# The attention layer of a four-layer graph network on one NeuronCore: heads on 96 rows, division after the running sums, paired 64-row products

## The chip, the cores and the metric

The kernel runs on one NeuronCore of a Trainium2 chip. The core has TensorE (PE, matrix products, with its weight loads shown as PEld), VectorE (DVE), ScalarE (ACT), GpSimd (POOL) and SyncE (SP, which here only issues DMAs). The metric is the time of one execution on the device, in microseconds. All data is 32-bit floating point, and every product on TensorE shows as two records in the trace; a transpose is one record.

## The reference

There are N = 50000 nodes with 64 scalars and 32 vectors of 3 components (D = 160 numbers) and E = 25000 edges, sorted by destination. Four layers follow one another (0 to 3), each with a part over edges and a part over nodes. Only layer 1, the attention layer, is touched (and the setup of the weights). It computes for every edge:

```python
s_n, v_n = layernorm of the scalars, RMS norm of the vectors of both end nodes
msg_s = (s_n @ Ws_src)[src] + (s_n @ Ws_dst)[dst]         # vectors alike
w1 = rbf @ W_rbf                                          # 16 radial numbers per edge
m1_s, m1_v = tensor_product(msg_s, msg_v, y0, y1, w1)     # y: 4 numbers per edge
a = sum over 16 of leaky_relu(m1_s @ W_alpha) * alpha_dot # one logit for each of 4 heads
amax = segment_max(a, dst);  ex = exp(a - amax[dst])
den = segment_sum(ex, dst);  alpha = ex / (den[dst] + 1e-16)
val_s, val_v = m1_s @ Ws_val, (m1_v @ Wv_val) * sigmoid(val_s @ Wg);  val_s = sigmoid(val_s)
m2_s, m2_v = tensor_product(val_s, val_v, y0, y1, w2)
h = [m2_s @ Ws_vlin, m2_v @ Wv_vlin]                      # 4 heads, 64 scalars, 32 vectors
agg = segment_sum(alpha * h, dst)
out = node + [agg_s @ Wps, agg_v @ Wpv]
```

## The kernel before

The edge part of the attention layer works on groups of 512 edges (`GE`), 50 groups (`NG`). After two transposes the features lie on partitions and the 512 edges along the free dimension, so a matrix product is 64 to 128 rows by 512 columns and a segment sum is a scan along the free dimension, carried from group to group. Sums of a destination are complete at its last edge; only that column's row is scattered to the table `aggregates`.

The groups are pipelined by hand. `steps1` runs a body for every step `s`, unrolled for the first 8, in a loop of two steps after that, and unrolled for 5 more at the end. In step `s` the engines work on several groups at once: group `s` is gathered, `s-1` is normalised (layer norm), `s-2` goes through the first products, `s-3` through values, gates and the logits, `s-4` through the softmax sums. Each engine carries out its own list of instructions in order, and semaphores (one for each kind of work, counted by group) tie the lists together. The names and lines are:

- **PE** (`attn_tensor`): transposes `NT0` to `NT2` (L872) of `normed`; products `MS`, `MV`; `AV` (logit inputs and values), `VV`, `GT`; `XS`, `XV`, `GS`, `GV`, which spread the 4 rows of `ex` and `dec` (partitions 64 to 67) over 64 and 96 rows; six products of `z_rows` (`B1` to `G`, 64 rows each); `PS`, `PV`; `US` (logits in its rows 64 to 67), `UV`; transposes R0 (L933) and R1 (L935) back; `HS`, `HV`. All products are recorded at L859, in the helper `mm`. Results go to one of 8 banks of PSUM; `ORDER` gives each name a place, place modulo 8 is its bank, and `bank_free` waits until the last user of the bank has been read.
- **DVE** (`attn_vector`): adds `h_s`, `h_v` (L958, L961); `z_rows` (L966); softmax on 4 rows: scan of the denominator `den` (L975), +1e-16 (L978), `dec` = den - ex (L979), reciprocal (L981), `ex` and `dec` times the reciprocal (L984, L985); layer norm statistics (L992, L993, L1000, L1004 to L1011); leaky ReLU (L1016); gate (L1022), `vy` (L1028); weighting (L1034, L1037) and the running sums, which are already normalised (L1042, L1048, with the decay in PSUM); the six products `pr` (L1059); `normed` (L1066); `neg` (L1073), running maximum (L1080) and its differences (L1084 to L1089); `xs_y`, `xv_y` (L1094, L1097).
- **ACT** (`attn_scalar`): copies from PSUM (`nt`, `m_s`, `m_v`, `val`, `us`, `uv`), tanh, the vector part of `normed` (L823), the exponentials (L838, L840), the copies into `agg_out` (L846, L847).
- **POOL** (`attn_gpsimd`): reciprocal root of the variances (L755, a power of -0.5), copies of indices (L763, L764, L780), eight gathers (L771) and four scatters (L785) for a group.
- **SP** (`attn_sync`): loads `z_in` (radial numbers and y rows, 256 KB) and `y_big` (768 KB) for each group.

The setup at the start of the program loads and scales the weights, zeroes the table `aggregates` (38 MB, from ACT's DMA queue) and builds `goes_on` (L429: 1 where an edge has the destination of the one before it) from 50 row loads of SP; layer 0 begins when that is done.

## Time and profile before

| | before |
|---|---|
| median of 3 runs | 5688.06 us (5687.17 to 5689.68) |
| profiled execution: time / span | 5691.12 us / 5689.3 us |
| PE busy | 4587.4 us, 81% of the span |
| DVE busy | 4072.7 us, 72% |
| POOL busy | 3297.1 us, 58% |
| ACT busy | 2192.9 us, 39% |
| mean granted clock of TensorE | 0.817 of full speed |

A busy share is an average over all stages. The edge part of layer 1, the only one that the change rewrites, reaches from 1311 us (first gather) to 3276 us (last scatter); the page's 40 slices of 142 us show where the engines are full, and windows, timelines and groups cut to that stretch show how one step goes. The granted clock is the share of its pulses that TensorE gets: 1.00 is 2.4 GHz, 0.50 is 1.2 GHz.

### The profile page before, as it was taken

The numbers are of one execution on the slowest core, as the hardware profiler recorded it, in microseconds if no ns is written. First come the engines' busy times: TensorE is split into PE (matmuls) and PEld (weight loads), VectorE is DVE, ScalarE is ACT, GpSimd is POOL, SyncE is SP. The second block draws the span as 40 slices with busy tenths as digits, with TensorE's granted clock in tenths as the row PEclk, the third lists the DMA queues.
The fourth block names the chain that finished last, engine by engine and source line by source line (L and its number), as shares of the span: only waits on it lengthen the run. The fifth ranks groups of instructions, "written<-read, shape, count | busy, mean of one in ns | idle before, by whom it ended". The sixth has DMA issues, their size and how long they took to land. (4 is left out here: it accounts for less than half of the span.)

```text
span 5689.3 us, 73586 instructions
## 1 busy us (share of the span) xinstructions
PE 4587.4 (81%) x14104; PEld 2009.0 (35%) x14104; DVE 4072.7 (72%) x10653; ACT 2192.9 (39%) x5204; POOL 3297.1 (58%) x3685
## 2 busy tenths in 40 slices
PE   0699987776999999999999900888879788887665
PEld 0233335552333333333333200333347533334554
DVE  1466659996887888787788787444459855556999
ACT  0223325553222222222222256333349833334555
POOL 0366669995344434443443244666657666667998
PEclk9999988787777777777777755898989899898877
DMA  9222227662222222122212199222249722225665
GB/s 363 81 67 67 68 56 226 215 216 71 52 56 52 53 52 56 51 54 51 56 50 50 28 344 339 62 66 66 66 136 356 275 63 69 66 67 152 196 192 162
DMA packets 545392, 678.01 MB, mean 119 GB/s; under 512 B 57166, under 2 KB 387106, under 8 KB 545052
## 3 DMA queue, kind: packets, MB, share of 16 engines
q1 hardware_dynamic: 451888, 496.01, 28.4%
q0 software_dynamic: 86400, 142.71, 9.1%
q10 hardware_dynamic: 7020, 38.40, 1.6%
q8 instruction: 25, 0.41, 0.0%
q14 instruction: 59, 0.48, 0.0%
HBM read 449.48 MB, written 245.49 MB: 122 GB/s over the span
## 5 line engine op out<-in xcount | busy, mean ns | idle before, releaser
L500 POOL DMA_INDIRECT aggregates<-agg_out,scatter_index x600 | 616.3, 1027 | 413.4 <-issue 253.3
L1231 ACT ACTIVATE y_chunk<-residual,ln_minus_mean_rstd,ln_rstd 128x160 f32<-128x160 f32 x1568 | 703.3, 555 | 377.3 <-POOL ln_minus_mean_rstd L1294 289.8
L755 POOL TENSOR_TENSOR edge_ln_rstd<-edge_ln_var,minus_half 128x16 f32<-128x16 f32 x50 | 146.9, 2938 | 854.6 <-DVE edge_ln_var L1011 854.6
L1197 PE MATMUL psum<-self_weights,x_chunk_T 128*128 128x160 f32 (+1 forms) x2352 | 491.9, 362 | 61.5 <-DVE node_mid L1322 29.3
L576 PE MATMUL psum<-identity,scaled_x 128*128 128x128 f32 x600 | 146.5, 282 | 486.0 <-DVE scaled_x L650 315.6
L1290 POOL TENSOR_TENSOR ln_rstd<-ln_var_eps,minus_half 128x4 f32<-128x4 f32 x392 | 441.0, 1125 | 145.3 <-DVE ln_var_eps L1379 85.7
L859 PE MATMUL psum<-rbf_times_sh,weights_layer 64*96 64x512 f32 (+1 forms) x600 | 513.7, 1040 | 2.4 <-DVE leaky_and_tanh L1016 1.6
L483 POOL DMA_INDIRECT gathered<-x_layer,gather_index x400 | 397.3, 993 | 176.2 <-issue 120.1
L1197 PEld LDWEIGHTS psum<-self_weights,x_chunk_T 128*128 128x128 f32 x2352 | 413.9, 224 | 108.1 <-issue 63.6
L1387 DVE BATCH_NORM_STATS2 ln_stats<-residual 128x6 f32<-128x160 f32 x1568 | 389.5, 308 | 0.1
L483 POOL DMA_INDIRECT gathered<-in_x,gather_index x200 | 207.5, 1038 | 229.3 <-DVE scaled_x L650 142.0
L599 PE MATMUL psum<-hidden,weights 64*128 64x512 f32 x300 | 185.6, 701 | 191.9 <-ACT hidden L534 140.8
L1275 POOL TENSOR_TENSOR agg_chunk<-agg_chunk,x_chunk 128x640 f32<-128x640 f32 x196 | 328.5, 1676 | 15.4
L675 DVE TENSOR_TENSOR products<-edge_weights,psum 128x512 f32<-128x512 f32 x150 | 103.2, 688 | 319.6 <-PE psum L603 311.2
L859 PE MATMUL psum<-message_products,weights_layer 96*96 96x512 f32 (+3 forms) x700 | 323.7, 606 | 0.0
L522 ACT ACTIVATE scaled_x<-gathered,sh_times_attr 128x160 f32<-128x160 f32 x400 | 138.4, 417 | 461.5 <-DVE sh_times_attr L633 310.1
L785 POOL DMA_INDIRECT aggregates<-agg_out,scatter_index x200 | 202.4, 1012 | 171.8 <-issue 88.5
L859 PEld LDWEIGHTS psum<-rbf_times_sh,weights_layer 64*96 64x96 f32 (+1 forms) x600 | 163.3, 281 | 322.7 <-issue 322.7
L576 PEld LDWEIGHTS psum<-identity,scaled_x 128*128 128x128 f32 x600 | 88.0, 147 | 489.2 <-ACT scaled_x L522 316.6
L1186 PE MATMUL psum<-identity,x_chunk 128*128 128x128 f32 x1176 | 224.5, 321 | 42.8 <-DMA agg_chunk<-aggregates 42.2
L1188 PE MATMUL psum<-identity,x_last_columns 128*128 128x128 f32 x294 | 97.7, 332 | 199.8 <-ACT x_last_columns L1238 199.5
L771 POOL DMA_INDIRECT gathered<-x_layer,gather_index x200 | 194.8, 974 | 88.8 <-issue 45.7
(202 smaller groups left out, 11059.7 us busy)
## 6 DMA issues: line engine op xcount, KB each, us to landing
x_layer<-y_chunk SPq DMA_DIRECT2D x294, 320.0 KB, 5.1
x_chunk<-x_layer SPq DMA_DIRECT2D x294, 320.0 KB, 4.7
agg_chunk<-aggregates SPq DMA_DIRECT2D x196, 320.0 KB, 5.5
sh_rows<-in_sh_big SPq DMA_DIRECT2D x50, 768.0 KB, 5.8
agg_chunk<-aggregates SPq DMA_DIRECT2D x98, 384.0 KB, 5.9
aggregates<-agg_out ACTq DMA_DIRECT2D x48, 768.0 KB
x_chunk<-in_x SPq DMA_DIRECT2D x98, 322.0 KB, 3.0
agg_chunk<-aggregates SPq DMA_DIRECT2D x98, 322.0 KB, 3.7
```

The costliest lines, as they stand in the source:

```text
L483: eng.indirect_dma_start(gathered[:, par, b, 0:width], None, x_table[l][:, :], bass.IndirectOffsetOnAxis(idx_src[:, par, b:b + 1], 0))\
L500: eng.indirect_dma_start(agg_table[:, :], bass.IndirectOffsetOnAxis(idx_last[:, q, b:b + 1], 0), agg_out[:, q, b, :], None, bounds_check=N ...
L576: eng.transpose(psum[:, TA, b * 128:b * 128 + 128], scaled[:, q, b, 0:128], ident[:, :])
L771: eng.indirect_dma_start(rows[:, par, b, 0:D], None, x_table[1][:, :], bass.IndirectOffsetOnAxis(idx[:, par, b:b + 1], 0))\
L785: eng.indirect_dma_start(agg_table[:, :], bass.IndirectOffsetOnAxis(idx_last[:, q, b:b + 1], 0), agg_out[:, q, b, :], None, bounds_check=N ...
L859: op = eng.matmul(pbank(name, rows), w, x, start=n == 0, stop=n == len(pairs) - 1)
L1186: eng.transpose(psum[:, 2 * q, b * 128:b * 128 + 128], x_in[:, buf, b, 0:128], ident[:, :])
L1197: eng.matmul(o[:, b, 0:ns + 96], x_t[:, k4, (2 * half + b) * 128:(2 * half + b) * 128 + 128], self_w[:, k, 0:ns + 96], start=b == 0, stop= ...
L1231: op = eng.activation(y_out[:, buf, b, :], res[:, buf, b, :], ACT.Identity, bias=shift[:, buf, b:b + 1], scale=rstd[:, buf, b:b + 1])
L1275: eng.tensor_tensor(rows, rows, x_in[:, buf, :, 0:D], ALU.add).then_inc(S["agg_x"], 1)
L1290: eng.tensor_tensor(rstd[:, buf, :], var_eps[:, q, :], minus_half[:, 0:T], ALU.pow)\
L1387: op = eng.bn_stats(stats[:, q, b, :], res[:, buf, b, :])
```

## The change

Head quantities get 96 rows: the product `AD` (weights: the logit column of each head repeated) puts every head's logit on 8 rows of each vector component, and `neg`, the running maximum, `dec`, `ex` and `den` are computed there on 96 partitions. The rows of the 64 head scalars are reordered in the weights (`Q1`, `HD`, `PS` of `head_w`), so that rows 0 to 63 of `ex` fit them; `XS`, `XV`, `GS`, `GV` go. The running sums take `ex` times h unnormalised and `dec` as the decay, and are multiplied at the end by the reciprocal of the denominator (`o_s`, `o_v`), which is formed on a spread layout, 128 x 16, reached by DMAs of SP: four from `den` to `den_t`, one to memory (`rden_d`), three back to `rden`. `PS` and `PV` go into the products R0 and R1, which take the place of the transposes.

Products over 64 rows are laid on both halves of the array (`B2`, `D`, `G` and half of `z_rows` in the upper one; `A1`/`V0`; `Q1`/`Q1`). The value scalars' part of the second tensor product comes from `q_y`, and h accumulates in PSUM (`HS`, `HV`). `z_rows` and `neg` move to POOL. The mean is taken out by the weights (`center`), the variance comes from sums on DVE and squares with accumulated outputs on ACT, and `normed` of a side is one instruction. POOL's loop is fully unrolled and takes its indices from the whole index arrays; the scatter moves from lag 5 to lag 6, and 7 steps follow the last group instead of 5. The setup has the further weights; the weights arrive in four DMAs.

```diff
+ORDER = [("NT0", 6, 2, "nt_copied", 3, 1), ("NT1", 4, ...), ("NT2", 0, ...), ("MS", 6, ...), ("MV", 4, ...),
+         ("AV", 0, 3, ...), ("VV", 7, 3, ...), ("GT", 6, 3, ...), ("AD", 5, 3, "a_less_max", 1, 1),
+         ("B1", 1, 2, "prods", 6, 1), ("B2", 2, ...), ("C", 3, ...), ("D", 6, ...), ("F", 4, ...), ("G", 0, ...),
+         ("HS", 7, 3, "hx_s", 1, 1), ("HV", 1, 3, "hx_v", 1, 1), ("R0", 2, 4, ...), ("R1", 3, 4, ...)]
 setup_sync:
+            eng.wait_ge(P["weights_in"], 64)
+            for name in ("B2", "D", "G"):
+                eng.dma_start(V(name)[upper, :], block(name, lower)).then_inc(P["head_in"], 16)
...
 attn_sync:
+                    for half in (0, 64):
+                        eng.dma_start(z_in[half:half + 64, par, :, :], t["rbf_sh"][:, cols].rearrange("(k p) e -> p k e", k=2))
+                if live(s, 4, NG):
+                    wait(eng, S["den"], c + 1)
+                    for h in range(4):
+                        eng.dma_start(den_t[32 * h:32 * h + 32, :], den[8 * h:8 * h + 1, par, :].rearrange("o (j i) -> o j i", j=32))
+                    wait(eng, S["rec"], c + 1)
+                    eng.dma_start(rden_d[:, :].rearrange("h (j i) -> (h j) i", j=32), rec[:, :])
+                    wait(eng, S["rec_out"], c * 16 + 16)
+                    for m in range(3):
+                        eng.dma_start(rden[32 * m:32 * m + 32, :], rden_d[:, :].unsqueeze(1).to_broadcast([4, 8, GE]))
+                if live(s, 1, NG):   # y_big as before, and y_pair, four rows spread over 64 partitions each
...
 attn_gpsimd:
+            for s in range(NG + 7):
+                if live(s, 2, NG):
+                    eng.tensor_tensor(z_rows[:, :], z_in[:, par, 0, :], z_in[:, par, 1, :], ALU.mult)
+                if live(s, 3, NG):
+                    eng.tensor_scalar(neg[:, :], goes_on[0:96, b_ * GE:b_ * GE + GE], -1.0, 1e30, ALU.add, ALU.mult)
+                if live(s, 0, NG):   # eight gathers, after applied and applied_v of s-2
+                if live(s, 1, NG):   # pow, after eps
+                if live(s, 6, NG):   # four scatters, after agg
 attn_scalar:
+                                eng.activation(normed[...], rows[:, q, b, 0:64], ACT.Square, scale=R8, accum_out=ln_e2[:, side, b, 0:1])
+                                op = eng.activation(normed[...], rows[:, q, b, 64:D], ACT.Square, scale=R32, accum_out=ln_e2[:, side, b, 1:2])
+                squares((0,))       # then val, tanh twice; squares((1, 2)); gate tanh; squares((3,))
 attn_tensor (b_ = s - 3, c = s - 4):
+                    eng.matmul(pbank("AV"), V("A1")[0:64, :], pr[0:64, 0, :], start=True, stop=False)
+                    eng.matmul(pbank("VV", 96), V("V0")[64:128, 0:96], pr[64:128, 0, :], start=True, stop=False)
...
+                    for name, n, lo in (("B1", 128, 0), ("B2", 128, 64), ("C", 96, 0), ("D", 96, 64), ("F", 96, 0), ("G", 96, 64)):
+                        eng.matmul(pbank(name, n), V(name)[lo:lo + 64, 0:n], z_rows[lo:lo + 64, :], start=True, stop=True)
+                    eng.wait_ge(S["qy"], at(S["qy"], 2 * b_ + 2))
+                    bank_free(eng, s, "HS")
+                    bank_free(eng, s, "HV")
+                    eng.matmul(pbank("HS", 64), X("Q1")[0:64, 0:64], q_y[0:64, 0, :], start=True, stop=False)
+                    eng.matmul(pbank("HV", 96), X("Q1")[64:128, 0:96], q_y[64:128, 0, :], start=True, stop=False)
+                    eng.matmul(pbank("HV", 96), X("Q2")[:, 0:96], q_y[:, 1, :], start=False, stop=False)
+                    eng.wait_ge(S["vy"], at(S["vy"], 4 * b_ + 4))   # then HD, H0, HF, HG
+                    for b in range(T):
+                        eng.matmul(pbank("R0")[:, b * 64:b * 64 + 64], o_s[:, b * 128:b * 128 + 128], X("PS")[0:64, 0:64], start=True, stop=True)
 attn_vector, in this order (g = s-1 for sums, squares, variance, eps, applied; s-4 for den, sums, o; s-3 for the rest):
+  sums (tensor_reduce x2) | den scan | hx_s, hx_v: ex * HS, ex * HV | scan_s, scan_v | wait den_t, rec = den_t + 1e-16
+  square | leaky | rec = 1 / rec | q_y x2 | wait rden, o_s, o_v | gated, vy x4 | variance
+  prods x6 (g = s-2, eps after the first) | wait rstd, applied x2 | carry, running maximum, carried, a_less_max, step
-                    eng.reciprocal(rden, rden).then_inc(S["rden"], 1)
-                            eng.bn_stats(ln_st[:, side, b, 0, :], rows[:, q, b, 0:64])
```

## Rows read from the trace of the kernel before

**Rows 1.** Page, part 2: TensorE's busy share, tenths, 40 slices of 142 us
```profile
PE   0699987776999999999999900888879788887665
```

**Rows 2.** Windows; columns us, busy (xcount) by engine, clock, DMA share, GB/s
```profile
1311.00:3276.00 1965.00, 1910.27 (x3900) 607.61 (x3900) 1544.53 (x3851) 523.22 (x1151) 784.78 (x800) 0.75 0.21 51
...
1349.80:1360.10 10.30, 4.65 (x15) 3.41 (x16) 6.10 (x16) 4.13 (x12) 8.03 (x8) 0.50 0.11 30
...
2203.00:2220.00 17.00, 17.00 (x25) 4.83 (x24) 11.49 (x23) 3.42 (x10) 12.19 (x16) 0.50 0.19 51
...
2220.30:2240.50 20.20, 20.20 (x56) 7.20 (x56) 19.00 (x56) 7.01 (x13) 3.22 (x3) 1.00 0.25 56
```

**Rows 3.** Timeline of PE: start us, us, engine, line, operation, shapes, count
```profile
2202.94 10.43 PE L859 MATMUL psum<-rbf_times_sh,weights_layer 64*128 64x512 f32 x12
...
1342.40 5.38 PE L859 MATMUL psum<-rbf_times_sh,weights_layer 64*128 64x512 f32 x12 [0.77 <-ACT message_vectors L805]
...
2236.25 2.09 PE L859 MATMUL psum<-exp_a,weights_layer 4*64 4x512 f32 x4
...
2224.68 1.48 PE L872 MATMUL psum<-identity,normed 128*128 128x128 f32 x12
```

**Rows 4.** Timeline of PE in the stage's filling, 1368 us
```profile
1368.12 0.67 PE L859 MATMUL psum<-jected_and_value_scalars,weights_layer 64*96 64x512 f32 x1
...
1368.13 0.69 PE L859 MATMUL psum<-rbf_times_sh,weights_layer 64*128 64x512 f32 x1
```

**Rows 5.** Groups by line, DVE, 1600 to 3000 us: count, busy us, mean ns, idle
```profile
L981 DVE RECIPROCAL reciprocal_denominator<-reciprocal_denominator 4x512 f32<-4x512 f32 x37 | 123.4, 3336 | 0.0
...
L1059 DVE TENSOR_TENSOR message_products<-message_vectors,psum 96x512 f32<-96x512 f32 x148 | 100.9, 682 | 113.7 <-PE psum L859 78.4 <-issue 34.9
...
L1080 DVE TENSOR_TENSOR_SCAN running_max<-segment_start_minus,running_max,psum 4x512 f32<-4x512 f32 x37 | 47.3, 1278 | 95.7 <-PE psum L859 68.1 <-issue 27.7
...
L1048 DVE TENSOR_TENSOR_SCAN running_vectors<-psum,running_vectors,vector_message 96x512 f32<-96x512 f32 x37 | 46.2, 1248 | 0.0
...
L993 DVE BATCH_NORM_STATS2 edge_ln_stats<-gathered 128x6 f32<-128x96 f32 x148 | 36.1, 244 | 0.0
...
L1000 DVE BATCH_NORM_AGGREGATE edge_ln_mean_var<-edge_ln_stats 128x2 f32<-128x6 f32 x576 | 42.0, 151 | 3.7
...
L1066 DVE TENSOR_SCALAR normed<-gathered,edge_ln_mean_var,edge_ln_rstd 128x64 f32<-128x64 f32 x148 | 36.3, 324 | 0.0
```

**Rows 6.** Groups by line, DVE, 300 to 1200 us
```profile
L641 DVE TENSOR_TENSOR scaled_x<-gathered,attr_of_src 128x256 f32<-128x256 f32 x40 | 17.1, 426 | 6.1 <-DVE sh_times_attr L633 4.1
```

**Rows 7.** Groups by line, POOL, attention stage; the last line from 3300 us on
```profile
L771 POOL DMA_INDIRECT gathered_dst<-x_layer,gather_index_dst x148 | 140.5, 949 | 46.7 <-issue 46.7
...
L785 POOL DMA_INDIRECT aggregates<-agg_out,scatter_index x148 | 149.0, 1007 | 67.3 <-issue 67.3
...
L755 POOL TENSOR_TENSOR edge_ln_rstd<-edge_ln_var,minus_half 128x16 f32<-128x16 f32 x36 | 105.8, 2938 | 631.3 <-DVE edge_ln_var L1011 631.3
...
L1281 POOL TENSOR_TENSOR node_features<-node_mid,node_gates 128x384 f32<-128x384 f32 x98 | 86.8, 886 | 93.7 <-ACT node_gates L1218 93.7
```

**Rows 8.** Groups by line, ACT, 1600 to 3000 us
```profile
L823 ACT ACTIVATE normed<-gathered,edge_ln_rstd 128x96 f32<-128x96 f32 x144 | 42.2, 363 | 129.2 <-POOL edge_ln_rstd L755 129.2
```

**Rows 9.** DMA issues (KB each, us to landing), and the timeline of the setup
```profile
x_chunk<-in_x SPq DMA_DIRECT2D x98, 322.0 KB, 3.0
...
3.77 2.14 SPq L332 DMA_DIRECT2D self_weights_tail<-in_weights  x4
```

**Rows 10.** Groups by line, DVE: 300 to 1200 us, then 3300 to 3560 us
```profile
L1379 DVE TENSOR_SCALAR ln_var_eps<-ln_mean_var 128x4 f32<-128x4 f32 x74 | 100.4, 1357 | 0.0
...
L1379 DVE TENSOR_SCALAR ln_var_eps<-ln_mean_var 128x4 f32<-128x4 f32 x91 | 14.8, 163 | 0.0
```

**Rows 11.** Timeline and waits of DVE in the setup
```profile
16.16 3.88 DVE L393 TENSOR_SCALAR weights<-weights 128x128 f32<-128x128 f32 x28 [16.16 <-DMA weights_layer<-in_weights]
...
DVE segment_goes_on L429 <- DMA dst_rows<-in_dst_row: 115.5, 46, 4.6
```

More of the change, by code:

```diff
@@ L244, in gnn_kernel @@
         EDGE = {0: conv_sems, 2: conv_sems, 3: conv_sems}
-        EDGE[1] = sems("edge1", "a_less_max agg aggr applied applied_v av_mm beta av_read back carried carry decay den "
-                                "den_e eps ex gate_t gated gather0 gather1 gs_mm gt_mm gv_mm hs hs_mm hv hv_mm "
-                                "hx_s hx_v index index_used leaky m_copied maxed ms ms_mm mv_mm neg gamma nt "
-                                "nt_copied p_copied p_mm prods rden rest rows0 rows1 rstd val scan_s scan_v "
-                                "scatter0 scatter1 square stats step us_mm us_y uv_mm uv_y vv_mm vy w_mm xs_mm "
-                                "xv_mm ys0 ys1 z")
+        EDGE[1] = sems("edge1", "a_less_max ad_mm agg applied applied_v av_mm carried carry decay den den_e den_t eps ex "
+                                "gate_t gated gather0 gather1 gt_mm hs_mm hv_mm hx_s hx_v leaky m_copied maxed ms_mm "
+                                "mv_mm neg nt nt_copied o_s o_v prods qy r_mm rden rec rec_out rows0 rows1 rstd "
+                                "scan_s scan_v scatter0 scatter1 square squares step sums th val variance vv_mm vy w_mm "
+                                "yq0 yq1 ys0 ys1 z")
         node_sems = sems("node", "act aggr agg_scaled agg_x applied eps feat gated half load0 load1 load2 load3 load4 load5 load6 load7 mid "
@@ L742, in step @@
-                    eng.dma_start(y_big[:, par, :, :], t["sh_big"][:, cols].rearrange("(k p) e -> p k e", k=4))\
-                       .then_inc(S["ys1"] if par else S["ys0"], 16)
-            steps(eng, NG, step, lead=8, lag=0)
+                    for half in (0, 64):
+                        eng.dma_start(z_in[half:half + 64, par, :, :],
+                                      t["rbf_sh"][:, cols].rearrange("(k p) e -> p k e", k=2))\
+                           .then_inc(S["rows1"] if par else S["rows0"], 16)
@@ L746, in attn_gpsimd @@
+            steps1(eng, step)
         def attn_gpsimd(eng):
@@ L853, in attn_tensor @@
             S = EDGE[1]
-            eng.wait_ge(P["bias"], 1)
-            def mm(name, rows, *pairs):
-                for n, (w, x) in enumerate(pairs):
-                    op = eng.matmul(pbank(name, rows), w, x, start=n == 0, stop=n == len(pairs) - 1)
-                return op
+            eng.wait_ge(P["head_ready"], 8)
             def step(s, par):
@@ new lines, in step @@
+                    eng.wait_ge(S["den_t"], at(S["den_t"], g * 64 + 64))
+                    wait(eng, S["rec_out"], g * 16)
+                    eng.tensor_scalar(rec[:, :], den_t[:, :], 1e-16, None, ALU.add).then_inc(S["den_e"], 1)
+                if live(s, 1, NG):
+                    g = s - 1
+                    eng.wait_ge(S["sums"], at(S["sums"], g + 1))
+                    wait(eng, S["variance"], g)
+                    eng.tensor_tensor(ln_sq[:, :, :], ln_sum[:, :, :], ln_sum[:, :, :], ALU.mult).then_inc(S["square"], 1)
@@ L1013, in step @@
                 if live(s, 3, NG):
                     g, q = s - 3, 1 - par
-                    eng.wait_ge(S["av_read"], at(S["av_read"], g + 1))
-                    eng.tensor_tensor(lk, lk, pbank("AV", 64), ALU.max).then_inc(S["leaky"], 1)
+                    eng.wait_ge(S["th"], at(S["th"], g + 1))
+                    wait(eng, S["yq1"] if q else S["yq0"], (g - q) * 32 + 64)
+                    wait(eng, S["hv_mm"], g)
+                    for k in range(2):
+                        eng.scalar_tensor_tensor(out=q_y[:, k, :], in0=th[:, :], scalar=1.0, in1=y_pair[:, q, k, :],
+                                                 op0=ALU.add, op1=ALU.mult).then_inc(S["qy"], 1)
```

545 lines of the change are left out of this document (286 added, 259 removed), and 13 rows, old and new, of the table ORDER.

## The prediction

> **What bounds the kernel now.** I read the page's slices first: PE is at 9 from the slice after 1300 us to 3200 us, through the attention stage, and nowhere else for so long [rows 1]. The window over the stage, 1311 to 3276 us, says what that means: PE busy 1910 of 1965 us, DVE 1545, POOL 785, ACT 523, mean clock 0.75 [rows 2]. There are 50 groups of 512 edges. The 37 groups counted in 1400 us on DVE [rows 5] give 37.8 us for a step; over the whole stage, without some 85 us of filling and 116 us of draining, it is 1762/46 = 38.3 us, which I use. PE runs 3900/50 = 78 records in it, and at half speed for a good part: 17 us at 0.50 and then 20 us at 1.00 [rows 2]. The six products of `z_rows` are the same twelve records in both: 10.43 us at half speed, 5.38 at full [rows 3]. Just before the fall come eight records whose operand has 4 rows (`exp_a`, `decay`) [rows 3]. So PE sets the step, and DVE's two large idle times, ahead of the products and of the running maximum, are both ended by PE [rows 5]; DVE, at 1545/1965 = 79%, stands right behind it: 31 us of work in each 38.3. A change must lower both.
>
> **DVE, part by part, for one step.** Durations are those of [rows 5]. Removed: the reciprocal on 4 rows, 3.3 us, with the four passes around it (+1e-16, `rest`, `beta`, `gamma`; 0.42 and three of 0.68 like any 512-wide product): 5.8 in all. `h_s`, `h_v` (1.4), the two additions of a bias (1.5), `z_rows` (0.7) and `neg` (0.5) go or move. Sixteen BATCH_NORM_STATS at 0.23 (0.24 over 96 elements, 0.21 over 64), sixteen aggregates (42.0/36 = 1.2) and eight `normed` at 0.32 go: 3.7 + 1.2 + 2.6; small operations 0.7. Removed: 18.1. Added: two sums and two wide `applied` of 256 elements, 0.43 each by L641 [rows 6]: 1.7; two `q_y` and two outputs `o_s`, `o_v`, four at 0.7: 2.8; five operations on 16 elements or fewer at 0.17: 0.9. Added: 5.4. Going from 4 to 96 rows costs nothing: the scan over 4 rows takes 1278 ns and the one over 96 takes 1248 [rows 5]. DVE work: 31.0 - 18.1 + 5.4 = 18.3, rounded up to 20 for handoffs.
>
> **PE.** 58 long and 20 short records become 50 long and 28 short (12 transposes, 16 of R0/R1). What matters is the pairing. In the stage's first steps the trace has a product on rows 64 to 127 (`WG`, starting 1368.12, 0.67 long) and one on rows 0 to 63 (`B1`, starting 1368.13, 0.69): the two run side by side, in the time of one [rows 4]. So the 12 records of `z_rows` need 6 slots, A1 with V0 two, and HS with HV on Q1 two: 40 slots at 5.38/12 = 0.45 us = 18.0, transposes 1.5 [rows 3], R0/R1 16 x 0.2 = 3.2: 22.7 us at full clock. If the pairing did nothing here it would be 50 slots, 27.2 us. The 4-row products are gone.
>
> **POOL** gets `z` (886 ns for 384 elements, hence 1.2) and `neg`, which no row shows (a one-input pass: between 0.2, the small copies, and 1.2, like `z`; I take 0.8), and keeps eight gathers at 1.25 us start to start (0.95 and a gap of 0.3), `pow` 2.9 and four scatters at 1.3 [rows 7]: 20.1 us. The index copies go with the unrolling. Its wait for `eps` now has the scatters, the next `z` and `neg` and the gathers behind it; gathers end 11 us before `sums` wants them. **ACT** gets 16 squares: at most 0.36 each by L823 [rows 8], 5.8 us. If each also costs a read of the accumulator (0 to 0.2 us, 0.2 being a small operation), 3.2 more: 14 to 18 us in all, off the path by about 3 us. If that cover went, they would delay `val`, hence `leaky`, by at most 2 us.
>
> **The new waits: three DMA hops in the middle of DVE's order.** `den` goes through SP to 128 partitions, is inverted, goes to memory and comes back on 96 rows. DVE's program waits in place for `den_t` and for `rden`, with everything of the step behind each wait. The nearest hop in the trace is 322 KB landing in 3.0 us [rows 9]; part of that is the payload, so 3.0 is the upper bound; half of it, 1.5, is the lower one, and I take 2.2 between them. Issuing one costs SP 2.14/4 = 0.5 us [rows 9]. Time 0 is the end of `applied` in DVE's order:
> - running maximum, three passes: 3.3; two exponentials on ACT: 4.5; scan of `den`: 5.8.
> - SP comes to `den` only after `z_in` of the next group, which waits for POOL's `z`: pow ends at -0.9, scatters 5.2, `z` 1.2: 5.5. Two issues, then four: 8.5 for the last, lands 10.7. DVE has its two products and two scans meanwhile (to 9.5), so it stalls 1.2.
> - small operations, `leaky`, reciprocal of 16 elements: 12.0. Write out 2.3: 14.3. Three reads, the last issued 1.0 later, landing 2.2 later: 17.5. Only `q_y` (1.4) lies in between, so DVE stalls some 4 us.
> - `o_s`, `o_v` 1.3, `gated` 0.7, `vy` 2.6, variance and first product 0.9: 23.0. `eps` 0.2, `pow` 2.9, handoffs 0.2 (five products run beside it), `applied` 0.9: 27.2.
> - DVE against POOL: DVE's 4-element addition at L1379 takes 1357 ns where POOL has long products and 163 where it has none [rows 10]: 1.2 lost for one meeting. `z` and `neg` fall on the scans, which have slack for part: 0.8.
>
> Step: 28.0 us. The shortest loop over PE is 22.8 (H products 5.2 after the bank of B1 is free, R 2.4, transposes 1.3, MS/MV 3.3 with their copies, AV/VV/GT 6.0, tanh, `gated`, `vy`, first product 4.6), so 5 us of slack are left for the clock. PE now idles 6 us before the H products, and after such a gap the trace has 10.3 us at 0.50, of which PE worked 4.65 [rows 2]: 2.3 us lost, inside the slack.
>
> One rule of the notes speaks against this change: the Trainium skill, page "SBUF — State Buffer", section "Who interferes with whom", says that a VectorE instruction with two SBUF inputs excludes a GpSimd instruction that reads SBUF, and here the scans and `o_v` become such. The 1357 ns agree in kind. By it up to 2.4 us of a step would be lost instead of 0.8, 78 us in all. The Trainium skill, "DMA: Bandwidth & Descriptors", section "Anatomy of one DMA", gives about 2.0 us fixed for a transfer from the GpSimd path; with it the three hops would come out 0.6 us shorter, 29 us in all. No run here has yet a small hop alone.
>
> **Setup.** SP now waits for the weights before anything else (landed at 16.16 [rows 11]) and issues 20 small DMAs at 0.5 to 0.6, 11 us, ahead of the loads that began at 2.5. All that SP issues after them, the row loads of `goes_on` at the end, starts 14 + 11 = 25 us later. DVE waits for those loads 46 times, 2.5 us in the mean and at most 4.6 [rows 11], the long waits being those beside the 38 MB of zeros that ACT's queue writes first. A start 25 us later means fewer groups at the long waits and more at the short ones, which gives back some of it: +18 us, between 0 and 28. Nothing hides it, for the first layer waits for the last of them.
>
> **The sum.** The profiled execution took 5691.1 us (span 5689.3), 3 over the median of 5688.1. 46 steps x (38.3 - 28.0) = 474; draining shrinks with the step, 116 x 0.23 = 27; setup +18. 5691 - 474 - 27 + 18 = 5208; on the median 5205. Each us of step is worth 48.6.
>
> **Rivals.**
> - A, shorter hops: hops of 1.5 us and `z` early give 24 to 25.5 us, PE and DVE near their own loops: 5010 to 5085. For it: 322 KB need only 3.0. Against: SP's issues remain. 0.15.
> - B, the clock or queueing eats the slack: two low stretches a step, or hops of 3 us behind the 1.3 MB of `sh` rows on the same queue, give 31 to 35: 5350 to 5545. For it: 17 us at 0.50 per step today though PE never rests [rows 2]. 0.17.
> - C, slower than before: PE stays at 0.50. Its part of the loop, 17.5 us, doubles: 22.8 + 17.5 = 40.3, so 41 with gaps: 5205 + 13 x 48.6 = 5837. It decides from the point where 0.9 of PE's time is at half speed. Against: all products but few have 96 or 128 rows busy, and such stretches ended the low clock at 2220 [rows 2]. 0.05.
> - D, the change doesn't do what it says: no pairing and both engines beside their waits add 4.5 to the PE loop, 27.3: no loss against the forecast, so it is inside it; the gain gone altogether (within 0.2%, 11 us, about what can be told from no change) 0.02.
> - The forecast, step 26 to 31 (5110 to 5350): 0.61.
>
> The range 5050 to 5450 is a step of 24.8 to 33, the bounds of hop, pairing and setup. Faster 0.93 (forecast, A, B), same 0.02, slower 0.05.
>
> **What would show it.** Starts of the vector scan 26 to 31 us apart; DVE idle 3 to 6 us a step ahead of `o_s`, ended by a DMA into the reciprocals, and under 2 ahead of `den_e`; twelve records of `z_rows` in about 2.8 us, in pairs; PE busy under 0.85 and clock over 0.85; the first layer beginning some 18 us later. Wrong would be: DVE stalls on PE instead (rival B or C), POOL never idle, or products that keep their 0.85 us a pair of records.

## The result and the profile after

The changed kernel takes 5536 us (median of four executions, 5515 to 5561), the kernel before 5688: a ratio of 0.9735, 95% interval 0.970 to 0.977. It is faster by 152 us; 483 were forecast, and 5536 lies outside the range of 5050 to 5450. The direction was right, the size was not.

The profiled execution was the fastest of the four: 5514.9 us, span 5513.0. Its busy totals, and the slices of PE and of the granted clock (40 slices, tenths), against [rows 1]:

```profile
PE 4147.5 (75%) x14102; PEld 1964.5 (36%) x14102; DVE 3527.4 (64%) x8554; ACT 2340.3 (42%) x6704; POOL 3407.0 (62%) x3639
PE   0499996775888877888888700888889788887777
PEclk9999997787878777787777655899989989998777
```

PE is at 7 to 8 through the attention stage where it was at 9, and the clock is at 7 to 8. No engine is full, yet the step is long. One group's scan of the vectors gives the step (operation, count, duration in ns, first and last start in us):

```profile
L1058 DVE TENSOR_TENSOR_SCAN running_vectors<-decay,running_vectors,vector_message x49: 1247/1252/1253, 1429.1 to 3145.0; 96x512 f32<-96x512 f32 x49
```

48 steps in 1715.9 us are 35.7 us each (35.6 with the first one), where 28.0 was forecast. The same scan in the kernel before:

```profile
L1048 DVE TENSOR_TENSOR_SCAN running_vectors<-psum,running_vectors,vector_message x49: 1245/1249/1278, 1444.7 to 3261.2; 96x512 f32<-96x512 f32 x49
```

That is 37.8 us a step (37.9 with the first one, which started at 1404.8); the forecast had reckoned with 38.3. From first gather to last scatter the stage took 1839 us instead of 1961.

By stage, the span's 176 us less are: setup +13, attention stage -122, the other three convolution stages -16, the stretches of the node parts between them -3, the last node part -48 (508 to 460 us). That last part is not touched by the change; in the profiled execution of every kernel below but one it is 507 or 508 again. So 122 us is what the rewritten stage gave in this execution.

**Where a step goes.** VectorE's waits from 1600 to 2900 us (us in total, times, longest):

```profile
DVE leaky_and_value_scalars L1072 <- ACT leaky_and_value_scalars L914: 234.5, 30, 10.9
DVE out_scalars L1092 <- DMA reciprocal_denominator<-reciprocal_denominators: 154.4, 36, 4.8
DVE vector_message L1052 <- PE psum L1008: 44.5, 26, 2.0
```

and TensorE's longest in the same stretch:

```profile
PE psum L1000 <- DVE message_products L1126: 217.1, 36, 6.6
```

One step in time, on DVE (start, duration, engine, line, operation; in brackets the idle time before it and its releaser):

```profile
2227.21 0.68 DVE L1072 SCALAR_TENSOR_TENSOR leaky_and_value_scalars<-leaky_and_value_scalars,psum 64x512 f32<-64x512 f32 x1 [7.67 <-ACT leaky_and_value_scalars L914]
2227.82 0.23 DVE L1077 RECIPROCAL reciprocal_spread<-reciprocal_spread 128x16 f32<-128x16 f32 x1
...
2234.40 0.68 DVE L1092 TENSOR_TENSOR out_scalars<-running_scalars,reciprocal_denominator 64x512 f32<-64x512 f32 x1 [4.51 <-DMA reciprocal_denominator<-reciprocal_denominators]
...
2238.97 0.68 DVE L1126 TENSOR_TENSOR message_products<-message_scalars,psum 128x512 f32<-128x512 f32 x1
```

and on PE in the same step, the head sums:

```profile
2203.37 1.93 PE L1000 MATMUL psum<-value_scalars_times_y,layer_head_weights 64*64 64x512 f32 x2 [6.28 <-DVE message_products L1126]
2205.24 2.02 PE L1001 MATMUL psum<-value_scalars_times_y,layer_head_weights 64*96 64x512 f32 x2
...
2214.55 1.27 PE L1008 MATMUL psum<-gated_times_y,weights_layer 96*96 96x512 f32 x2
```

Three things are to be seen. First, each engine waits for the other in turn. PE's head sums wait for DVE's first product (they write the bank it reads). DVE's `leaky` waits for the value copy, which comes after the head sums, the transposes, MS and MV and A1/A2 on PE. The reciprocal stands behind `leaky`, and so do the two hops, the division, the gate, `vy` and the next first product. Added up for this step: head sums 12.4, sums into rows and transposes 3.5, to the end of A2 6.4, value copy 1.6 (1.0 of it behind four squares), `leaky` and reciprocal 0.85, hops to `out_scalars` 6.35, from there to the first product 4.6, to the head sums 0.8: 36.4 us in one chain. Second, L1000 and L1001 are the half-height pair that was to run side by side, and they run one after the other. Third, PE is slow there (us of the window; busy us per engine; granted clock; DMA):

```profile
2201.40:2215.00 13.60, 11.63 (x13) 2.89 (x14) 12.35 (x21) 3.38 (x10) 10.11 (x8) 0.50 0.50 123
2215.00:2235.50 20.50, 16.89 (x66) 7.62 (x64) 6.63 (x11) 10.11 (x43) 7.72 (x8) 1.00 0.25 66
```

The clock is at its lower level, 1.2 of 2.4 GHz, for 13.6 us of this step; the low stretches of the stage are 13.7 us in the median and up to 23.9.

### The profile page after: what moved, and what is told of

Read it like the earlier page. It is cut to its first block and busy times, and to the rows that moved or that the text cites. A ratio compares the mean times of both kernels' runs of the same rounds, so it can differ in the third digit from the quotient of the medians.

```text
span 5513.0 us, 73349 instructions
## 1 busy us (share of the span) xinstructions
PE 4147.5 (75%) x14102; PEld 1964.5 (36%) x14102; DVE 3527.4 (64%) x8554; ACT 2340.3 (42%) x6704; POOL 3407.0 (62%) x3639
## 5 line engine op out<-in xcount | busy, mean ns | idle before, releaser
L548 POOL DMA_INDIRECT aggregates<-agg_out,scatter_index x600 | 615.0, 1025 | 402.6 <-issue 254.8
L531 POOL DMA_INDIRECT gathered<-x_layer,gather_index x400 | 397.7, 994 | 176.2 <-issue 115.3
L1000 PE MATMUL psum<-value_scalars_times_y,layer_head_weights 64*64 64x512 f32 x100 | 95.9, 1060 | 294.2 <-DVE message_products L1126 290.3
L862 POOL DMA_INDIRECT aggregates<-agg_out,last_index x200 | 209.2, 1046 | 95.0 <-issue 56.7
L931 ACT ACTIVATE normed<-gathered,edge_ln_rstd 128x96 f32<-128x96 f32 x200 | 58.5, 362 | 488.1 <-POOL edge_ln_rstd L853 488.1
L845 POOL DMA_INDIRECT gathered<-x_layer,src_index x200 | 220.9, 1104 | 67.1 <-issue 58.5
L1072 DVE SCALAR_TENSOR_TENSOR leaky_and_value_scalars<-leaky_and_value_scalars,psum 64x512 f32<-64x512 f32 x50 | 34.0, 679 | 353.4 <-ACT leaky_and_value_scalars L914 308.5
L876 ACT ACTIVATE normed_T<-psum 128x512 f32<-128x512 f32 x150 | 85.5, 593 | 367.4 <-PE psum L956 320.2
```

Source lines behind the costliest of these rows:

```text
L531: eng.indirect_dma_start(gathered[:, par, b, 0:width], None, x_table[l][:, :], bass.IndirectOffsetOnAxis(idx_src[:, par, b:b + 1], 0))\
L548: eng.indirect_dma_start(agg_table[:, :], bass.IndirectOffsetOnAxis(idx_last[:, q, b:b + 1], 0), agg_out[:, q, b, :], None, bounds_check=N ...
L845: eng.indirect_dma_start(rows[:, par, b, 0:D], None, x_table[1][:, :], bass.IndirectOffsetOnAxis(idx[:, col:col + 1], 0))\
L862: eng.indirect_dma_start(agg_table[:, :], bass.IndirectOffsetOnAxis(last_i[:, col:col + 1], 0), agg_out[:, par, b, :], None, bounds_check= ...
```

## The experiments

All edits are of the changed kernel unless a text says otherwise. "Step" is the mean distance of the 50 vector scans in the profiled execution; times are medians.

### One edit at a time

**Padding.** HS gets 96 columns.

```
-eng.matmul(pbank("HS", 64), X("Q1")[0:64, 0:64], q_y[0:64, 0, :], start=True, stop=False)
+eng.matmul(pbank("HS", 96), X("Q1")[0:64, 0:96], q_y[0:64, 0, :], start=True, stop=False)
...
-eng.matmul(pbank("HS", 64), X("HD")[0:96, 0:64], vy[:, 1, :], start=False, stop=True)
+eng.matmul(pbank("HS", 96), X("HD")[0:96, 0:96], vy[:, 1, :], start=False, stop=True)
```

> The two products that the scalar head sums take are padded from 64 to 96 output columns (the added columns multiply zeros). In the changed kernel the pair L1000 (rows 0 to 63, 64 columns) and L1001 (rows 64 to 127, 96 columns) ran one after the other: each took two slots of 0.9 us at half clock, with a bubble between them. Theory: two half-height products run side by side only where their column counts are of one kind, so with 96 columns on both sides the second starts 0.1 us after the first, and the H products take 2 us less of a step at half clock: step 33.6 instead of 35.6 us, total about 5440. Rival: they are kept apart by something else (the accumulation in two banks, the wait ahead of them), and nothing moves: step 35.6 us, total 5515 to 5560.

Measured: 5322 us, step 30.3 us. More work, 214 us less. Its head sums on PE:

```profile
2212.54 1.13 PE L1000 MATMUL psum<-value_scalars_times_y,layer_head_weights 64*96 64x512 f32 x1 [4.82 <-DVE message_products L1126]
2212.54 1.17 PE L1001 MATMUL psum<-value_scalars_times_y,layer_head_weights 64*96 64x512 f32 x1
```

They now start together. The gain of 5.3 us a step is more than the expected 2: the head sums (L1000 to L1008 on PE) fell from a median of 12.8 to 8.4 us, since the low stretch also shrank, from 13.7 to 6.8 us in the median (here 6.20 us at 0.50):

```profile
2212.30:2218.50 6.20, 5.96 (x9) 1.95 (x10) 5.86 (x12) 2.23 (x8) 5.21 (x3) 0.50 0.90 219
2218.50:2242.00 23.50, 19.03 (x70) 8.30 (x68) 14.13 (x23) 11.04 (x45) 12.84 (x12) 1.00 0.27 71
```

The control keeps the padding and puts the product of Q2 between the two (start flags moved with it):

> Padding as in e1_pad_hs, but the product of Q2 stands between the two half-height products, so that they cannot run side by side, while every product of the head sums keeps 96 columns. If padding gained by the pair: the head sums take one product of two slots more (0.9 us at full, 1.8 us at half clock) and the step is 1 to 2 us (and what the clock adds, up to 5.3 us in all) longer than 30.3 us, total 5370 to 5540. If it gained because the column count no longer changes between products: the step stays at 30.3 us, total 5320.

Measured: 5501 us, step 34.6 us:

```profile
2226.23 1.99 PE L1000 MATMUL psum<-value_scalars_times_y,layer_head_weights 64*96 64x512 f32 x2 [6.22 <-DVE message_products L1126]
2228.15 2.02 PE L1001 MATMUL psum<-value_scalars_times_y,layer_head_weights 128*96 128x512 f32 x2
```

So of the 5.3 us, 4.2 come with the pair, the clock's share of it included, and 1.1 with the padding even without a pair. The 1.1 is read from one profiled execution of each; the four executions of this control lie up to 70 us apart, which is 1.4 us a step, so it isn't told from nothing. The 4.2 is.

**The reciprocal first.** The block of four lines with `eng.reciprocal(rec...)` moves from behind `leaky` to ahead of it.

> The reciprocal of the denominators stands ahead of the leaky maximum in VectorE's program instead of behind it; nothing else changes. Theory (the step is one serial loop: products, head sums, transposes, message sums, value copy, leaky maximum, reciprocal, two DMA hops, division, gate, times y, products): the hops then run beside TensorE's work, the idle time of 4.3 us ahead of out_scalars (L1092) goes, the gate starts 4.4 us earlier, at the end of tanh_gates. With the clock as it is: step 31.2 us, total about 5345. If the shorter idle time of TensorE ahead of the head sums also keeps its clock at full speed, they take 6 instead of 12.4 us: step 26 to 28 us, total about 5150 to 5200. Rival (the clock alone makes the step long, the division is covered anyway): the idle time moves to the next wait and the step stays at 35.6 us.

Measured: 5430 us, step 33.0 us. The wait for the reciprocals is gone from DVE's list; what is left there is the chain over PE, and the clock went down with it:

```profile
DVE leaky_and_value_scalars L1076 <- ACT leaky_and_value_scalars L914: 326.4, 37, 8.9
DVE vector_message L1052 <- PE psum L1008: 69.0, 37, 2.0
...
1600.00:2900.00 1300.00, 1210.99 (x2974) 510.20 (x2974) 803.18 (x1344) 520.68 (x2024) 710.63 (x577) 0.70 0.35 89
```

The mean clock fell from 0.78 to 0.70, with low stretches of 20.5 us in the median. The loop theory holds in kind (the wait of 4.3 us goes, the step shortens by 2.7), and neither of the two sizes expected was right: with the clock as it was, 4.4 us were expected. That the clock took the difference is read from the longer low stretches and was not tried by itself.

**TensorE kept busy.** Ahead of the z product G:

```
+if name == "G" and B:
+    for _ in range(4):
+        eng.matmul(pbank("G"), ident[:, :], head_w[:, 0:4, :].rearrange("p b c -> p (b c)"),
+                   start=True, stop=True)
```

> Four products of 128 x 128 by 512 whose result is overwritten at once are added on TensorE ahead of the last z product (G), where TensorE otherwise waits 6.3 us for VectorE. They add work and shorten no wait. Clock theory: the granted clock stays at full speed over the head sums, which take 6 instead of 12.4 us, so step 29 to 30 us, total about 5250. Rival (the clock follows something else, or the added work delays the z products as much): step 35.6 us or up to 39 us, total 5520 to 5700.

Measured: 5404 us, step 32.3 us, clock 0.88 from 1600 to 2900 us. The head sums take 6.8 us in 17 of the 40 steps there and 11.5 us or more in most others. Work of no use makes the kernel 133 us faster: the clock is in the chain. It gives 3.3 us of the 6 expected, for 29 low stretches remain in those 40 steps (324 us of the 1300, against 556).

**GpSimd's two products late.** `z` and `neg` move behind the gathers.

> GpSimd does its z product and its negation behind the eight gather launches of the step instead of ahead of them. In the changed kernel VectorE's scan of the denominators (L1045), which runs beside them, took 2.19 us, the other scans about 1.28. Contention theory: the scan takes 1.3 us; since TensorE's head sums, not the scan, set the time of what follows, the step moves by less than 0.5 us. Rival 1 (the scan itself is slow because both its inputs are in SBUF): it stays at 2.2 us. Rival 2: the late z product or negation holds up TensorE's z products or the maximum scan, and the step grows by 1 to 5 us.

Measured: 5740 us, step 38.9 us: slower even than the kernel before, by 0.9% (0.7 to 1.1). The contention is there, as the scan of the denominators shows (changed kernel first, then this one; durations are least, median, most in ns):

```profile
L1045 DVE TENSOR_TENSOR_SCAN denominator<-decay,denominator,exp_a x37: 2142/2153/2236, 1600.0 to 2882.7; 96x512 f32<-96x512 f32 x37
```

```profile
L1045 DVE TENSOR_TENSOR_SCAN denominator<-decay,denominator,exp_a x33: 1279/1280/1350, 1630.3 to 2890.5; 96x512 f32<-96x512 f32 x33
```

But `z` frees the buffer for the next load of `z_in`, which stands ahead of the denominators' transfers in SyncE's program. So SyncE waits, and the hop with it; its waits and DVE's:

```profile
SPq L302 <- POOL rbf_times_sh L842: 513.8, 28, 19.3
```

```profile
DVE reciprocal_spread L1063 <- DMA denominator_spread<-denominator: 389.7, 33, 14.2
```

389.7/33 = 11.8 us a step. In the changed kernel SyncE waits for `z` too, 6.9 us a step (254.1 us in 37 times), but there the hop isn't what VectorE waits for. This rival had been named for the z products on PE; it came over the DMA queue instead.

**Head weights from ScalarE's queue.** The twenty transfers of the setup are issued there.

> The twenty transfers of the head weights are issued from ScalarE's queue instead of SyncE's; nothing else is changed. Theory: the changed kernel's setup is 12.9 us longer because SyncE issues them ahead of the index and column loads; segment_goes_on then ends at about 189.5 instead of 202.4 us and the total is 13 us (0.23%) less, 5500 to 5545. Rival 1: the row loop is paced by something else and the setup keeps its 202 us. Rival 2: VectorE waits for the head weights even longer, as ScalarE's issues are slower: 210 us.

Measured: 5586 us, 50 more than the changed kernel. The setup does what was expected (the building of `segment_goes_on`, changed kernel and this one; the last start is the number):

```profile
L477 DVE TENSOR_TENSOR segment_goes_on<-dst_rows x50: 684/692/694, 76.8 to 202.4; 128x512 int32 x44, 128x512 uint8<-128x512 int32 x6
```

```profile
L477 DVE TENSOR_TENSOR segment_goes_on<-dst_rows x50: 684/693/693, 28.2 to 189.4; 128x512 int32 x44, 128x512 uint8<-128x512 int32 x6
```

The 13 us come back, and later stages of the profiled execution take 95 more: the attention stage 1865 us instead of 1839 (from 1600 to 2900 us the low stretches are 20.5 us in the median), the convolution of layer 2 another 15, the last node part 507 instead of 459 (below), which is half of the 95 and not shown to come from the edit.

### Edits on top of the padding

> Padding of the scalar head sums (step 30.3 us alone) and the reciprocal ahead of the leaky maximum (33.0 us alone) together. In the padded kernel VectorE still waits 5.1 us a step for the spread reciprocals ahead of out_scalars (L1092). Serial-loop theory: that wait goes, step 25.2 us, total 5100 or so; TensorE has 24.4 us of work in such a step and is then the bound. Rival (the clock takes it back, as it did with the reciprocal moved alone, where the half-clock stretch grew from 13.7 to 20.5 us): the stretch grows from 6.8 to about 14 us, step 28 us, total about 5230. Third: nothing on top of the padding, step 30.3 us, total 5320.

Measured: 5233 us, step 28.6 us: the number of the first rival, but not by its cause. That rival (clock) asked for stretches of 14 us; they stayed at 6.8. The wait that was to go is still there, for another reason:

```profile
2206.96 0.17 DVE L1063 TENSOR_SCALAR reciprocal_spread<-denominator_spread 128x16 f32<-128x16 f32 x1 [1.70 <-DMA denominator_spread<-denominator]
...
2214.66 0.68 DVE L1092 TENSOR_TENSOR out_scalars<-running_scalars,reciprocal_denominator 64x512 f32<-64x512 f32 x1 [4.44 <-DMA reciprocal_denominator<-reciprocal_denominators]
```

The value copy no longer holds anything up. What is left is the loop over DVE and the hops, the forecast's own 28.0 us loop; the two experiments that shorten the hops and leave them out, below, bear this out. From the end of the scan (2201.72) to L1063 are 5.2 us, and SyncE's issues are a good part of it:

```profile
2202.39 2.49 SPq L792 DMA_DIRECT2D denominator_spread<-denominator  x4
2207.49 0.36 SPq L799 DMA_DIRECT2D reciprocal_denominators<-reciprocal_spread  x1
2209.31 2.01 SPq L805 DMA_DIRECT2D reciprocal_denominator<-reciprocal_denominators  x3
```

**Squares last.** All three calls of `squares` stand behind `tanh_gates`.

> As the kernel before it in this set, and the sixteen squares of ScalarE all stand behind tanh_gates, so that the value copy (L914) no longer waits for the first four (1.0 us in the trace) nor tanh_gates for the next eight. If the loop still runs through the value copy: 1.0 us a step less, total 50 us less than with two edits. If TensorE is the bound: no difference, or some loss where the squares now end later than GpSimd's power wants its variance.

Measured: 5246 us, step 28.7: no gain. The value copy is off the loop: in the kernel without this edit VectorE's waits for it come to 5.2 us in 9 times from 1600 to 2700 us, against 234.5 in 30 times in the changed kernel.

**Padding and TensorE kept busy.**

> Padding and the four products of no use ahead of the last z product. With padding alone the head sums still ran half at low clock (8.4 us, low stretch 6.8 us a step). Clock theory: the low stretch goes, the head sums take 6 us, step 27.9 us, total about 5210. Rival (little idle is left to fill, and the added 3.4 us of products stand ahead of the head sums): step 30.3 to 32 us, total 5320 to 5400.

Measured: 5268 us, step 29.2. The mean clock is 0.96 and the head sums take 6.0 us in the median, as expected, but the step gives 1.1 us, not 2.4: DVE waits 5.4 us a step for the spread reciprocals (215.9 us in 40 times). At nearly full clock the chain over the hops sets the step.

**Products early.** The loop over the six products is split; B1, B2 and C go ahead of `out_scalars`.

> Padding and the reciprocal first (step 28.6 us), and the first three of the six message products (B1, B2, C) are taken ahead of out_scalars in VectorE's program, inside its wait of 4.4 us for the spread reciprocals. Theory: the loop that is left runs over VectorE and the two hops (denominator scan, spread, reciprocal, spread, division, gate, times y, products, maximum scan, exponentials, denominator scan), so three products of 0.6 us leave it: step 26.8 us, total about 5140. TensorE also starts its head sums without a wait for the product B1. Rival (TensorE's 24.4 us at its clock is what bounds): 28 us or more, total 5200 to 5230.

Measured: 5264 us, step 29.1: 0.4 worse. Waits of DVE, 1600 to 2700 us:

```profile
DVE normed L1142 <- POOL edge_ln_rstd L853: 72.9, 38, 2.0
DVE message_products L1093 <- PE psum L994: 66.2, 40, 3.9
...
DVE out_scalars L1100 <- DMA reciprocal_denominator<-reciprocal_denominators: 54.4, 24, 2.8
```

The three products had been the cover of GpSimd's power (2.9 us): without them `normed` waits 1.9 us for it, and the products wait 1.7 us for PE. The gain became two new waits. TensorE's head sums didn't start without a wait either; only the instruction that ends it is another, the gate's, which reads the other bank they write:

```profile
PE psum L1000 <- DVE gated_vectors L1107: 141.7, 37, 5.1
```

**One transfer for the denominators** instead of four, with padding and the reciprocal first:

```
+eng.dma_start(den_t[:, :], den[0:32:8, par, :].rearrange("h (j i) -> h j i", j=32))\
+   .then_inc(S["den_t"], 16)
```

> Padding and the reciprocal first (step 28.6 us), and the spread of the denominators goes as one transfer instead of four; 0.6 us of SyncE's issue for each of the four stand in the trace between the scan and reciprocal_spread (L1063), 5.2 us in all. Same theory of the loop: 1.8 us leave it, step 26.8 us, total about 5140. If one transfer of 128 short rows lands later than four of 32, less. Rival (the hops are not in the loop any more): 28.6 us, total 5230.

Measured: 5187 us, step 27.6: 1.0 of the 1.8 us. The scan of the denominators of one step ends at 2206.33, and L1061 follows 4.4 us later instead of 5.2:

```profile
2204.10 2.23 DVE L1043 TENSOR_TENSOR_SCAN denominator<-decay,denominator,exp_a 96x512 f32<-96x512 f32 x1 [0.56 <-issue]
...
2210.70 0.18 DVE L1061 TENSOR_SCALAR reciprocal_spread<-denominator_spread 128x16 f32<-128x16 f32 x1 [0.82 <-issue]
```

Over the stage this stretch is 4.2 us in the median instead of 5.2, and the step falls by as much: the hops are in the loop. SyncE's issue falls from 2.49 to 0.61 us, so some 0.9 us of the saving are given back between the issue and the use of the one transfer of 128 short rows.

**All together, and neg late.**

> Padding, reciprocal first, three products early, one transfer for the denominators, and the head weights issued from ScalarE's queue. Loop theory: 28.6 less 1.8 less 1.8 = 25.0 us a step, near TensorE's own 23 to 24.4 us, setup 13 us less: total about 5230 - 175 - 13 = 5040. Rival: TensorE bounds or loses its clock and the step stays at 26 to 27 us: 5090 to 5140.

> As the kernel before it in this set, and GpSimd's negation alone (not its z product, which held up SyncE when both were moved) stands behind the gather launches. The scan of the denominators then runs beside the z product alone: 1.28 us where nothing runs beside it, 2.15 where both do, about 1.7 here. Theory: it is now in the loop, so the step is 0.4 us shorter, total 20 us less. Rival: z product alone covers the scan in time and nothing moves, or the negation now comes too late for the maximum scan and the step grows.

Measured: 5231 us, step 29.4, and 5182 us, step 27.8. Of the 4.4 us by which the first misses its 25.0, 1.7 are the early products' own harm: without them the same kernel has 27.7 (last experiment). The other 2.7 are savings that were counted and didn't come: 1.8 for the early products, 0.8 for the one transfer. In the second the scan still takes 2.25 us, so `z` alone covers it, and the expected cause did not act. The step is 1.6 us shorter all the same, and VectorE's wait for PE ahead of the early products is down from 108.7 us (45 times) to 44.5 (22 times) between 1600 and 2700 us; why was not settled.

### The division left out

In two kernels the denominators' transfers, the reciprocal and both waits for them are removed.

> The division by the running denominators is left out of the changed kernel: no transfer of the denominators, no reciprocal, and out_scalars and out_vectors multiply by a constant tile of ones. Loop theory: the wait of 4.3 us ahead of out_scalars goes as it did with the reciprocal moved, and one transfer-bound wait (L1063, 0.5 us) too: step 31 us if TensorE's low stretch stays at 13.7 us; 33 us if it grows to 20.5 us as with the reciprocal moved alone (33.0 us). Rival (the hops cost the step more than their waits show, by the queue of SyncE): under 30 us.

> Padding, and the division left out in the same way. With padding and the reciprocal first (28.6 us) VectorE still waits 4 us ahead of out_scalars. If the hops are the last part of the loop: 25 us a step or less, total about 5050. If TensorE's work and clock bound by then (24.4 us of work at clock 0.88): 26.5 to 28 us, total 5120 to 5200.

Measured: 5379 us, step 32.4, clock 0.71, and 5003 us, step 24.9. The second from 1600 to 2600 us (busy us of PE, its weight loads, DVE, ACT, POOL; clock):

```profile
1600.00:2600.00 1000.00, 893.56 (x3099) 384.14 (x3097) 815.93 (x1308) 521.21 (x2074) 699.99 (x582) 0.96 0.43 108
```

Unpadded, leaving the division out gives 3.2 us, 0.6 more than moving the reciprocal alone: what remains there is PE's part of the chain, with the head sums unpaired and at low clock (VectorE waits 8.9 us a step for the value copy), and for that loop the round trip need only be out of the way. Padded, it gives 5.4 us, and TensorE is busy for 894 of 1000 us at clock 0.96; its longest wait, for VectorE's products, is 2.3 us a step.

### The version that beats both

Padding, reciprocal first, one transfer, head weights from ScalarE's queue.

> Padding, reciprocal first, one transfer for the denominators, head weights issued from ScalarE's queue; no product taken early. Step as in e12_one_dma, 27.6 us, and setup 13 us less: total 5187 - 13 = 5174. Rival: the earlier start shifts the phases of the engines and the stage takes back more than the 13 us, as it did with the head weights moved alone (step 36.1 instead of 35.6 us): 5190 to 5230.

Measured: 5126.5 us in five executions (5120 to 5130), ratio to the kernel before 0.9005 (0.899 to 0.902): 410 us faster than the changed kernel. The step is 27.7 us. The 48 us beyond what was expected are luck: the last node part took 459 us here and 508 in the kernel that the sum started from.

## Why the prediction was wrong, point by point

**The step that failed** is "Step: 28.0 us. The shortest loop over PE is 22.8 [...], so 5 us of slack are left for the clock". The forecast drew two loops side by side, one over DVE and the hops (28.0) and one over PE (22.8), and took the longer. In the program they are one. The bullet "small operations, `leaky`, reciprocal of 16 elements: 12.0" took `leaky` as ready. Its input comes at the end of PE's head sums, transposes and message sums, and since the reciprocal stands behind it in DVE's order, the hops, the division, the gate and the next first product start only then. The PE loop as forecast ended at `tanh`, `gated`, `vy`; the measured one has the 6.35 us of hops inside. Moving four lines (33.0 us) and leaving the hops out (32.4) both show it. The sum closes too: to the forecast's 22.8 the head sums add 7.2 (12.4 for 5.2) and the hops 6.35, which gives 36.35, and the step read above has 36.4 (the other terms differ from the forecast too, but cancel to 0.1 us). Of the signs that the prediction named for being wrong, the first, DVE stalling on PE, came: 7.7 us ahead of `leaky` in that step, ended by ScalarE's copy of what PE had just finished.

With both causes mended by padding and the reciprocal first, the step is 28.6 us, and the 28.0 us loop bounds only then. That the two numbers lie so close is partly luck: the hops take 12.4 us where 10.4 were forecast (5.2 and 7.2 instead of 4.9 and 5.5), and `leaky`, 0.7 us, no longer stands between them.

**The clock**: "2.3 us lost, inside the slack". There was no slack, and the low stretch was 13.7 us in the median, not 10.3; the head sums alone took 12.8 instead of 5.2 in the median, through the clock and the missing pair; paired and at nearly full clock they still take 6.0. Rival B (two low stretches a step or hops of 3 us, step 31 to 35, 5350 to 5545 us, 0.17) has the measured time inside it and the measured step a little beyond it. Its heading, that the clock eats the slack, is half of what happened; its form is not: there were 51 low stretches in 50 steps, longer ones and not two a step, and no slack beside the hops to eat. The stated range ended at a step of 33 and so left out the upper half of this rival.

**The pairs**: [rows 4] showed one pair, of 96 and 128 columns, and the forecast gave the same to every half-height pair. For z (twelve records in 2.86 us at full clock, 2.8 forecast), A1/V0 and WG/AD it holds. For HS/HV, 64 and 96 columns, it does not: the count of 40 slots was two too low, worth 4.2 us a step once the clock is counted.

**DVE, POOL, ACT work** in a step, from the busy time of 1600 to 2900 us over 36.5 steps: DVE 760/36.5 = 20.8 (20 forecast), POOL 18.2 (20.1), ACT 13.4 (14 to 18). Right, or a little less than forecast. **The accumulator read** is an instruction of its own of 0.19 us (0 to 0.2). **Contention** on the denominators' scan 0.87 us (0.8), and off the chain in this kernel. **The hops**: from the scan's end to `den_t` 5.2 us (with padding and the reciprocal first; 4.9 forecast), from the reciprocal's end to `out_scalars` 6.35 in the step read above and 7.2 with padding and the reciprocal first (5.5). Too short by 1.2 to 2.0 us in sum; the issues weigh 0.6 us each, not 0.5, and the shorter hops that the prediction also considered would have missed by more. **Setup** +12.9 (18, 0 to 28). **The 18.1 us less of DVE work** brought little because DVE was no longer what the step waited for: of the 10.3 us forecast for a step, 2.3 arrived (37.9 to 35.6).

**The sum** itself has two small slips. The step before was 37.9 us between scans, not 38.3, which is 18 us over 46 steps. And the part by which the draining shrinks, 1 - 28.0/38.3, is 0.27 and not 0.23, 31 us instead of 27. With measured terms the 49 distances between the 50 scans give 49 x (37.89 - 35.62) = 111 us of the stage's 122; filling and draining gave the rest.

## What to carry to other kernels

When work on several engines goes round in one loop, follow one value through the program order of every engine: an instruction that needs nothing late but stands behind one that does joins two short loops into a long one, and that costs more than any instruction saved. Before a pair of partial-height products is counted as one, look for a pair of the very same row and column counts in the trace. An engine's work taken away is worth only what the chain passes through it; and any cheap, early step that stands on a shared in-order queue (SyncE's here) has to be checked before it is moved.

## What was not expected of the hardware

- **The column counts decide whether a pair forms.** Two products on rows 0 to 63 and 64 to 127 run side by side with 96 and 96 columns (both started at 2212.54), also with 128 and 96 (both at 2223.53 in the changed kernel), and one after the other with 64 and 96. No other count below 96 was tried. Padding with zeros made the kernel 214 us faster.
- **Less idle time alone is not what raises the clock.** Ahead of the head sums PE idles 2.3 us in the median with the reciprocal moved alone and 2.8 us with padding as well, and in a whole step 2.3 and 4.2 us; the low stretches are 20.5 and 6.8 us, the shorter ones where the idle time is longer. What separates them was not settled. Useless products raised the clock in both cases where they were tried.
- **Two gears of an untouched part.** The last node part takes 508 us or 460 us. In the short form (the changed kernel, first fence) GpSimd's power over 4 elements takes 1017 ns and VectorE's small pass 132; in the long form (head weights moved, second fence) 1672 and 1305:

```profile
L1348 POOL TENSOR_TENSOR ln_rstd<-ln_var_eps,minus_half x98: 1006/1017/1599, 5077.9 to 5505.5; 128x4 f32<-128x4 f32 x98
L1425 DVE TENSOR_SCALAR angle_whole_turns<-angle_turns x98: 128/132/1282, 5061.1 to 5491.7; 128x8 f32<-128x8 f32 x98
```

```profile
L1348 POOL TENSOR_TENSOR ln_rstd<-ln_var_eps,minus_half x98: 1007/1672/1681, 5111.3 to 5587.4; 128x4 f32<-128x4 f32 x98
L1425 DVE TENSOR_SCALAR angle_whole_turns<-angle_turns x98: 129/1305/1315, 5094.6 to 5571.5; 128x8 f32<-128x8 f32 x98
```

  The two engines fall into step with one another in one of two ways, and a shift of some us in an earlier stage seems to choose; what chooses was not tried. It may differ between executions of one kernel as well: with everything together they took 5201, 5203, 5259 and 5266 us. Only one execution of each was profiled, so this is not shown. Differences near 48 us between two kernels here say nothing of the edit.
- The Trainium skill, page "SBUF — State Buffer", section "Who interferes with whom", has a VectorE instruction with two SBUF inputs and a GpSimd instruction that reads SBUF exclude each other. The scan of the denominators agrees: 2153 ns beside GpSimd's products and 1280 without; the later scans of the same step, beside launches of gathers alone, take 1252 either way.
